# Three moves in the hand-written order of a gated delta sublayer: kk before y and the chunk join after the output projection on TensorE, a round of convolution taps before the output normalization on VectorE

## The reference, cut to what matters

```python
q = silu(dwconv_causal(x @ Wq)); k = silu(dwconv_causal(x @ Wk)); v = silu(dwconv_causal(x @ Wv))  # 4 taps
alpha = sigmoid(x @ Wa + ba); beta = sigmoid(x @ Wb + bb)
def step(S, qt, kt, vt, at, bt):            # over the 256 tokens, for each batch and head
    err = einsum('bhvk,bhk->bhv', S, kt) - vt
    S = at * S - bt * err[..., None] * kt[:, :, None, :]
    o = einsum('bhvk,bhk->bhv', S, qt)
o = layernorm(o) * ln_w + ln_b
o = (o * sigmoid(x @ Wg)) @ Wo
```

## Time and profile before

| | before |
|---|---|
| median of 3 runs | 3861.36 us |
| lowest, highest | 3859.85, 3864.56 us |
| the profiled execution | 3864.56 us |
| its span, first to last instruction | 3862.8 us |
| mean granted TensorE clock | 0.945 |
| TensorE busy | 3488.6 us (90%) |
| VectorE busy | 2372.1 us (61%) |
| ScalarE busy | 1895.2 us (49%) |
| GpSimd busy | 773.5 us (20%) |

### The profile page before, as it was taken

One profiled execution on the slowest core, in us unless ns is written; L12 is line 12 of the kernel. 1 busy time (PEld: TensorE's weight loads), 2 busy tenths in 40 slices (PEclk: granted clock), 3 DMA queues, 4 the chain that ended last, 5 costly groups with the idle time before them and its releaser, 6 DMA issues. The chain is left out here.

```text
span 3862.8 us, 89209 instructions
## 1 busy us (share of the span) xinstructions
PE 3488.6 (90%) x35196; PEld 2815.5 (73%) x35196; DVE 2372.1 (61%) x6031; ACT 1895.2 (49%) x4673; POOL 773.5 (20%) x797
## 2 busy tenths in 40 slices
PE   4999987999999999999997789998899977769998
PEld 3777755888888888888886467776688855547887
DVE  2666645778777787777775256665455445545554
ACT  1555523666666666666663045554444323334442
POOL 1232211223222222222222022322000011110000
PEclk8999967999999999999998599999999988989999
DMA  2000020000000000000000220000000000000000
GB/s 90 1 1 1 1 114 20 16 22 16 22 16 22 24 22 19 19 19 19 19 21 8 67 81 1 1 1 1 1 1 1 1 1 1 1 1 1 1 1 23
DMA packets 56949, 67.24 MB, mean 17 GB/s; under 512 B 11092, under 2 KB 46166, under 8 KB 54998
## 3 DMA queue, kind: packets, MB, share of 16 engines
q1 hardware_dynamic: 56534, 61.53, 5.1%
HBM read 59.22 MB, written 2.29 MB: 16 GB/s over the span
## 5 line engine op out<-in xcount | busy, mean ns | idle before, releaser
L1164 DVE SCALAR_TENSOR_TENSOR d_acc<-d_raw,d_taps,d_acc 128x255 f32<-128x255 f32 (+2 forms) x1152 | 642.8, 599 | 146.8 <-ACT d_raw L1154 133.2
L1389 ACT COPY d_power<-bank 128x768 f32<-128x768 f32 x320 | 259.1, 810 | 218.7 <-PE bank L1382 218.7
L2168 ACT ACTIVATE m_probs<-bank,m_nmax 128x128 f32<-128x128 f32 (+1 forms) x512 | 166.3, 436 | 266.3 <-DVE m_nmax L2160 266.3
L1152 ACT ACTIVATE d_acc<-bank,d_tap_bias,d_taps 128x256 f32<-128x256 f32 x384 | 196.0, 561 | 166.8 <-PE bank L1133 166.7
L536 POOL TENSOR_TENSOR a_q<-a_rope 64x512 f32<-64x512 f32 x128 | 163.3, 1276 | 318.0 <-DVE a_rope L526 276.3
L526 DVE TENSOR_TENSOR a_rope<-bank,a_sinT 32x512 f32<-32x512 f32 x256 | 177.4, 693 | 5.7
L576 ACT ACTIVATE a_probs<-bank,a_nmax 128x128 f32<-128x128 f32 x256 | 93.6, 366 | 168.3 <-DVE a_nmax L567 168.3
L513 PE MATMUL bank<-a_latT,a_wq 128*128 128x256 f32 x512 | 168.5, 411 | 6.9 <-DVE a_rope L526 4.5
L603 ACT COPY a_probsT<-bank 128x512 f32<-128x512 f32 (+1 forms) x260 | 137.3, 580 | 55.6 <-PE bank L594 54.6
L1192 POOL TENSOR_TENSOR d_qT<-d_acc,d_sigm 128x512 f32<-128x512 f32 x64 | 84.4, 1318 | 375.6 <-ACT d_sigm L1174 375.6
L184 POOL TENSOR_TENSOR rstd<-var_eps,minus_half 128x2 f32<-128x2 f32 x66 | 47.1, 714 | 554.3 <-DVE var_eps L166 532.7
(11 more groups left out here) (293 smaller groups left out, 9383.9 us busy)
## 6 DMA issues: line engine op xcount, KB each, us to landing
d_alpha<-d_alpha_rows SPq DMA_DIRECT2D x64, 256.0 KB, 3.5
d_g_decay<-d_running_rows SPq DMA_DIRECT2D x32, 258.0 KB, 3.5
a_w_o<-in_a_w_o SPq DMA_DIRECT2D x2, 2048.0 KB
a_q_nope<-in_a_q_nope SPq DMA_DIRECT2D x2, 1536.0 KB
x<-in_x SPq DMA_DIRECT2D x8, 256.0 KB, 4.4
d_wk<-in_d_wk SPq DMA_DIRECT2D x1, 2048.0 KB
d_wq<-in_d_wq SPq DMA_DIRECT2D x1, 2048.0 KB
d_wv<-in_d_wv SPq DMA_DIRECT2D x1, 2048.0 KB
```

Source lines behind the costliest of these rows:

```text
L1152: nc.scalar.activation(acc[:, r % 3, j], b_proj[:, j * T:(j + 1) * T], ACT.Identity, scale=taps[:, r // 2, h, 3:4], bias=tap_bias[:, r // ...
L1164: last = nc.vector.scalar_tensor_tensor(out=acc[:, r % 3, j, d:T], in0=raw[:, r % 2, j, 0:T - d], scalar=taps[:, r // 2, h, 3 - d:4 - d], ...
L1389: nc.scalar.copy(power[:], b_step[:, :, 0:3 * P]).then_inc(g.step_out, 1)
L2168: last = nc.scalar.activation(probs[:, s % 2, i, cols], heads[:, i, cols], ACT.Exp, bias=nmax[:, s % 2, t, i:i + 1])
```

## The change

In TensorE's list `kk_pe(u + 1)` stands before `y_pe(e)` instead of behind it. Also in TensorE's list, `join_pe(u)` stands behind `out_pe(e)` and `xnT_pe` instead of ahead of them. In VectorE's list the round of taps 1 (even units) or 4 (odd units) stands between `o_stats_dve(e)` and `o_normal_dve(e)` instead of behind `o_normal_dve(e)`. No instruction is added, removed or altered, and ScalarE's and GpSimd's lists stay as they are.

```diff
--- before.py
+++ after.py
@@ -1606,10 +1606,10 @@
                     live = u < UNITS
                     if live:
                         step_pe(pe, u, 0)
+                    if u + 1 < UNITS:
+                        kk_pe(pe, u + 1)
                     if e >= 0:
                         y_pe(pe, e)
-                    if u + 1 < UNITS:
-                        kk_pe(pe, u + 1)
                     if n == CHUNKS - 2 and u + 2 < UNITS:
                         ab_pe(pe, u // CHUNKS + 1)
                     if live:
@@ -1646,12 +1646,12 @@
                         corner_pe(pe, u)
                     if q is not None:
                         project_pe(pe, q + 3)
-                    if live:
-                        join_pe(pe, u)
                     if e >= 0:
                         out_pe(pe, e)
                     if n == CHUNKS - 3 and u + 3 < UNITS:
                         xnT_pe(pe, u // CHUNKS + 1, q + 4)
+                    if live:
+                        join_pe(pe, u)
 
             @block.vector
             def _(dve):
@@ -1686,10 +1686,10 @@
                         ab_dve(dve, u // CHUNKS + 1)
                     if e >= 0:
                         o_stats_dve(dve, e)
+                    if ahead is not None:
+                        taps_dve(dve, ahead, 1 if u % 2 == 0 else 4)
                     if e >= 0:
                         o_normal_dve(dve, e)
-                    if ahead is not None:
-                        taps_dve(dve, ahead, 1 if u % 2 == 0 else 4)
                     if u % 2 == 0 and ahead is not None:
                         silu(dve, ahead, 0)
                     if e >= 0 and e % 2 == 0:
```

## The result

The changed kernel takes 3963.69 us in the median (four runs, 3958.11 to 3967.0) where the kernel before takes 3860.61 beside it: ratio 1.0268, 95% interval 1.0247 to 1.0288. It is slower by 103 us. The profiled execution took 3967.43 us, its span is 3965.7 us.

What follows compares the result with a forecast made beforehand. TensorE's own instruction order was taken to bound the kernel. The sum 3864.6 + 34 + 66 + 27 = 3992 us, less 3 us for the slow profiled execution, gave 3989 us for the median, range 3952 to 4030.

Steps and rivals of the forecast that it cites:

- the first rival: Delta loop: TensorE dense around the new wait, so the clock does not fall; 3965 us, chance 0.2.
- TensorE's order sets the pace, with one hole: Delta loop: TensorE streams without gaps except 30 waits of 0.4 us before `corner_pe`; reordering wins at most 11.7 us.
- Part 1: TensorE, `kk_pe` ahead of `y_pe`: costs 0 in every unit, bounds 0 and 19 us.
- Part 2: TensorE, `join_pe` behind `out_pe`: step 0 waits for the join's copy, 0.53 us a unit, 34 us in all.
- Part 3: VectorE, taps ahead of `o_normal_dve`: odd units 0; late `o_n` costs 30 even units 2.21 us each, 66 us.
- The clock: TensorE after the new even-unit waits: 17 falls to half clock, 1.6 us each, 27 us, bounds 0 and 51.

Runs made afterwards that it cites:

- taps_odd: Kernel before with the taps round moved ahead of `o_normal_dve` in odd units alone: 3860.6 us against 3858.87, ratio 1.0001.
- k_copy_late: Kernel before with ScalarE's `k_act` moved behind `step_act(u, 5)` in even units: 3849.34 us against 3858.87, ratio 0.9972.
- join: Kernel before with only `join_pe` moved behind `out_pe` and `xnT_pe`: 3890.42 us against 3858.08, ratio 1.0086.
- taps: Kernel before with only the taps round 1 or 4 moved ahead of `o_normal_dve`: 3984.84 us against 3858.08, ratio 1.0331.
- taps_join: Changed kernel with `kk_pe` left behind `y_pe`, so only taps and `join_pe` moved: 3964.42 us, ratio 1.0278.
- kq_late: Changed kernel with `kg` and `qg` moved behind `og` on GpSimd: 3914.17 us against 3858.87 for the kernel before, ratio 1.0141.

## Why the prediction was right, and where it was not

The direction, the place and the mechanisms held. The forecast was 3989 us, 128 us slower; measured are 103, within the range. The time itself fell on the value of the first rival, no fall of the clock (3965). This is partly luck of terms that cancel: the rival's two parts add up to 100 us, and measured they are 97, with 9 us of clock and 1 of the end on top and 5 us less behind the loop:

- *TensorE's order sets the pace, with one hole.* Right. taps_odd fills VectorE's wait for nothing, and k_copy_late removes the hole and brings 10 us.
- *Part 1, 0 us.* Right for the change. Alone it is 2.7 us by the unit lengths (4 us by the medians) through a wait of kk that I had not listed.
- *Part 2, 34 us.* Mis-sized: 0.43 us a unit, not 0.53, so 26 us for units 1 to 61; join alone measured 32 us in all by the medians, 30.6 by unit lengths to unit 62, since there an even unit pays 0.57 us. Join to step 0 is 1.01 us, more than the 0.91 forecast. But the eight matmuls of the last projection take 1.83 us instead of 1.92 with `out_pe` behind them (1207.02 to 1208.85 in the timeline of after), and those of `out_pe` 1.82 instead of 1.92 with the join behind them. Why they are shorter there was not found. From the projection's start to step 0: 1.92 + 0.38 + 1.92 = 4.22 before, 1.83 + 1.82 + 1.01 = 4.66 after.
- *Part 3, odd units 0, even units 2.21 us, 66 us.* Right: 2.29 us in 23 units, 2.67 in the seven with the gates, 71 us. The taps took 4.18 us, forecast 4.1; `oT_pe` waited 2.68 us, forecast 2.6. What I left out: in the gate units VectorE's extra work makes `o_var` late, so the pow, `kg` and `qg` start later and more of them falls on the taps (4.56 us at 1199.26 in the timeline of after).
- *The clock, 27 us.* This is the term that was most off: six falls, not 17, 9.1 us and not 27. The step that failed was to carry the share of 8 in 14 from one stretch to another. The same wait is followed by a fall in 28, 14, 6 or 4 of 30 units, depending on what else is moved. By the Trainium skill ("TensorE: Matmul & The Clock Gate", section "HAM oscillation — how this bites in real kernels") a loop with a long enough wait in each pass pays in every pass. The taps alone come near that with 28 of 30, the changed kernel does not.
- Sum of the terms as measured: 26 + 71 + 9 + 1 for the end = 107, less the 5 us of the untouched rest: 102. The spans of the two profiled executions differ by 102.9, the medians by 103.1.

## What to carry to other kernels

When one engine's own order is the pace, ask of each instruction that is moved two things: what it waits for at the new place, and what its reader did with the time in between; a producer moved right ahead of its consumer lays open the whole round trip (here about 1 us through one copy). Idle time on an engine that isn't the bound is a margin: filled with work that itself has to wait, it makes everything behind it late. And a small hole in the pacing engine, found in its list of waits, was worth more than the three moves: two lines on ScalarE, 10 us.

## What the runs showed of the hardware

- The same wait of TensorE, 2.7 us (3.1 in the units with the gates), 30 times in a loop, was followed by a fall to the half clock 28 times in one order (taps) and 4 to 6 times in another that differs by 0.4 us in each unit (taps_join, the change). Waits of up to 1.2 us (kq_late) and of 0.6 us (join) were followed by none. A fall of 3.4 us cost 1.3 to 1.6 us, one of 6.8 us 2.6 to 2.8.
- Two-input operations of VectorE on SBUF beside such operations of GpSimd are not slowed evenly: six taps take 2.70 us alone, 4.18 beside `kg` and `qg`, 5.44 beside `og`, `kg` and `qg` (kq_late). The pow on four columns of GpSimd did not lengthen them (2.70 us, taps_odd).
- At full clock, eight projection matmuls with 256 columns take a slot of 1.83 us with 128-row matmuls behind them (1.86 ahead of `out_pe` in the even units of join) and 1.92 us with the 64-row ones of a step or of the join behind them. The eight of `out_pe` do not follow this: with the join behind them they take 1.82 us in the changed kernel, and in the run join 1.82 in odd units and 1.92 in even ones.
